# The tail of a two-layer transformer kernel: a loop over stages replaced by an order written out call by call, one of two roundings moved to ScalarE, and the factors of the pairs taken out of rings

## The reference, cut to what matters

```python
scores = einsum('bthd,bshd->bhts', wq, wk) / sqrt(8)
attn   = einsum('bhts,bshd->bthd', softmax(scores), wv)
x      = x + tanh(g_xattn[1]) * (attn @ wo.T + bo)
...
def qlinear(x, w, b):                         # rows of x scaled to -127..127 and rounded
    scale = 127.0 / clip(max(abs(x), -1), EPS)
    xq = clip(round(x * scale), -128, 127)
    return (xq @ wq.T) / (scale * sw) + b     # wq is -1, 0 or 1
h   = layernorm(x, gamma, beta)               # 128 wide
h   = gelu(qlinear(h, w1, b1))                # 512 wide
x   = x + tanh(g_ffn[1]) * qlinear(h, w2, b2)
```

## Time and profile before

| | |
|---|---|
| median of 3 runs | 430.23 us |
| the profiled execution, its time | 430.68 us |
| its span, first to last instruction | 428.9 us |
| granted TensorE clock, mean over the span | 0.976 |
| busy: PE, DVE, ACT, POOL | 90%, 77%, 60%, 53% |
| last exp of the phase starts on ACT | 379.84 us |
| last store is issued | 426.68 us |

### The profile page before, as it was taken

How to read it: one execution, slowest core, us unless ns; L and a number is a source line. 1 busy time by engine, 2 the same in 40 slices (tenths; PEclk the granted TensorE clock), 3 DMA queues, 4 the chain that set the end, 5 groups by cost and what they waited for, 6 DMA issues and landing times. The chain is left out here.

```text
span 428.9 us, 10603 instructions
## 1 busy us (share of the span) xinstructions
PE 383.9 (90%) x3641; PEld 282.8 (66%) x3654; DVE 332.2 (77%) x933; ACT 255.9 (60%) x506; POOL 226.7 (53%) x372
## 2 busy tenths in 40 slices
PE   8799989999999999999999999988888887765765
PEld 7356656666666666786578887856666766654554
DVE  3789998999989998885738874665588888866772
ACT  2478757777777777766542224445777676773252
POOL 4575497566666666632300002773788887656021
PEclk9999999999999999999999999999999999975799
DMA  5889999100000000000000000000000000000011
GB/s 160 245 146 136 135 125 127 14 3 2 2 2 2 2 2 2 0 2 2 2 2 0 0 2 2 0 2 2 2 2 3 2 2 2 2 2 0 16 38 49
DMA packets 61284, 13.29 MB, mean 31 GB/s; under 512 B 51488, under 2 KB 60592, under 8 KB 61232
## 3 DMA queue, kind: packets, MB, share of 16 engines
q1 hardware_dynamic: 59776, 11.94, 18.8%
q10 hardware_dynamic: 1328, 0.66, 0.5%
q0 software_dynamic: 128, 0.00, 0.0%
HBM read 11.55 MB, written 1.05 MB: 29 GB/s over the span
## 5 line engine op out<-in xcount | busy, mean ns | idle before, releaser
L397 POOL TENSOR_TENSOR a_rn<-a_ssq,neghalf 128x8 f32<-128x8 f32 x48 | 79.0, 1655 | 30.1 <-DVE a_ssq L996 25.6
L996 DVE TENSOR_REDUCE a_ssq<-q_home 128x8 f32<-128x512 f32 x48 | 32.3, 673 | 6.4 <-ACT q_home L783 6.3
L486 PE MATMUL a_x<-wkv_a,a_kvT 128*128 128x512 f32 x64 | 34.5, 621 | 0.9 <-ACT kv_home L789 0.8
L91 POOL TENSOR_TENSOR moments<-moments,eps_row 128x1 f32<-128x1 f32 x32 | 6.2, 195 | 54.9 <-DVE moments L86 54.6
L789 ACT ACTIVATE kv_home<-a_x,maskcol 128x512 f32<-128x512 f32 x32 | 21.9, 684 | 18.4 <-PE a_x L486 18.4
L1750 DVE TENSOR_REDUCE b_mx<-b_s 128x16 f32<-128x1024 f32 x16 | 19.6, 1225 | 10.4 <-PE b_s L1461 10.3
L1338 POOL TENSOR_TENSOR b_k<-b_ksb,quad 128x256 f32<-128x256 f32 x32 | 19.0, 614 | 14.3 <-ACT b_ksb L1625 14.3
L1015 DVE TENSOR_REDUCE a_mx<-a_s 128x4 f32<-128x512 f32 x32 | 22.0, 686 | 2.0 <-PE a_s L512 1.9
L413 POOL TENSOR_TENSOR a_yr<-a_ymv,eps_row 128x1 f32<-128x1 f32 x16 | 3.1, 192 | 38.0 <-DVE a_ymv L1039 38.0
L801 ACT ACTIVATE kv_home<-a_m,cols 128x512 f32<-128x512 f32 x32 | 22.0, 686 | 0.8 <-PE a_m L500 0.7
L531 PE MATMUL a_m<-kv_home,p_home 128*64 128x65 f32 x512 | 22.0, 228 | 0.3 <-ACT p_home L811 0.3
(11 more groups left out here) (293 smaller groups left out, 1186.7 us busy)
## 6 DMA issues: line engine op xcount, KB each, us to landing
w_gu<-in_L_ffn_Wg_dram SPq DMA_DIRECT2D x4, 512.0 KB, 9.1
w_gu<-in_L_ffn_Wu_dram SPq DMA_DIRECT2D x4, 512.0 KB, 11.1
w_d<-in_L_ffn_Wd_dram SPq DMA_DIRECT2D x8, 256.0 KB, 7.8
out_dram<-xs SPq DMA_DIRECT2D x8, 128.0 KB, 1.8
xs<-in_x_dram SPq DMA_DIRECT2D x1, 640.0 KB, 11.4
cs<-in_ctx_dram SPq DMA_DIRECT2D x1, 640.0 KB, 10.9
wkv_a<-in_L_xattn_Wkv_dram SPq DMA_DIRECT2D x1, 512.0 KB, 8.4
nat<-in_L_ffn_w_dram SPq DMA_DIRECT2D x2, 256.0 KB, 3.1
```

Of the source, the lines that this page charges most:

```text
L397: nc.gpsimd.tensor_tensor(rn[:, tp, i, :], ssq[:, tp, i, :], neghalf[:, 0:H0], ALU.pow)\
L486: nc.tensor.matmul(p_x[:], kvT[:, tp, b * 2 * S:(b + 1) * 2 * S], wkv_a[:, INNER:2 * INNER], start=True, stop=True).then_inc(vproj_done, 1)
L996: nc.vector.tensor_reduce(ssq[:, tp, i, :], sq[:, i, :].rearrange("p (h d) -> p h d", h=H0), AX.X, ALU.add).then_inc(reduced, 1)
```

## The change

1. In all four loops the stages behind the attention's last exp are cut off, and the calls that remain are written out one by one, in an order of their own for each engine.
2. The two idle matmuls of `turn_hidden` become a call of their own, `keep_busy(j)`. It is called ten times (three times for pair 0, once for each other pair), where before there were eight; the first stands ahead of `up(11)`.
3. Of each pair, the odd tile is rounded by ScalarE (`round_out`), the even one by VectorE as before. `turn_hidden` waits for a semaphore of each.
4. The factors of the second half have a column for each tile (`top2`, `fine2`, `back2`, 128x16) in place of the rings of two pairs, and the waits that guarded the rings are gone.

The number and the size of all other calls is the same.

```diff
+        top2 = sb("top2", [P, NT])
+        fine2 = sb("fine2", [P, NT])
+        back2 = sb("back2", [P, NT])
...
             def hidden_back(j):
                 pool.wait_ge(g_bound, j + 1)
-                wait(pool, x_done, j - 1)
...
-            for s in range(3, NT + 4 + NP):
+            for s in range(3, NT + 3):
...
+            norm_back(12)
+            add_bias(15, 1)
+            add_bias_2(0)
+            inverse_root(13)
+            norm(13, 1)
+            add_bias_2(1)
+            norm_back(13)
+            add_bias_2(2) ... add_bias_2(5), hidden_back(0), add_bias_2(6), hidden_back(1)
+            inverse_root(14), norm(14, 0), hidden_back(2), hidden_back(3), inverse_root(15), norm(15, 1)
+            norm_back(14), hidden_back(4), add_bias_2(7), norm_back(15), hidden_back(5), (6), (7)
...
-            def turn_hidden(j):
+            def keep_busy(j):
                 if j < 2:
                     pe.wait_ge(shifted, NT)
                 wait(pe, gT_ready, j - 1)
                 busy(nc, p_s[:, 2 * (j % 2), 0:256], ident[:], v["wq_a"][:, 0:256], 2)
-                pe.wait_ge(g_rounded, 2 * j + 2)
+
+            def turn_hidden(j):
+                wait(pe, gT_ready, j - 1)
+                pe.wait_ge(g_rounded, j + 1)
+                pe.wait_ge(g_odd_rounded, j + 1)
...
+            def round_out(t):
+                act.wait_ge(g_fine, t // 2 + 1)
+                nc.scalar.activation(hid[:, t, :], hid[:, t, :], ACT.Copy, bias=MAGIC, scale=fine2[:, t:t + 1])\
+                    .then_inc(g_odd_rounded, 1)
...
             def hidden_largest(j):
                 dve.wait_ge(gelu_done, j + 1)
-                wait(dve, g_back, j - 1)
```

More of the change, by code:

```diff
@@ L1572, in _ @@
             pe.wait_ge(zeroed, 3)
-            for s in range(1, NT + 4 + NP):
+            for s in range(1, NT + 1):
                 if s == 3:
@@ L1585, in _ @@
                     up(s - 6, s % 2)
[L1586 to L1589, removed]
                 if exists(s - 3, NT):
@@ L1602, in _ @@
                     mix(s - 2, s % 2, 0)
+            mix(14, 0, 1)
+            keep_busy(0)
+            up(11, 1)
+            probs_T(15, 1, 0)
+            probs_T(15, 1, 1)
+            turn_attention(14, 0)
+            keep_busy(0)
+            keep_busy(1)
+            out_proj(14, 0)
+            turn_norm(12, 0)
+            mix(15, 1, 0)
+            mix(15, 1, 1)
+            keep_busy(0)
+            turn_hidden(0)
+            turn_hidden(1)
+            turn_attention(15, 1)
+            up(12, 0)
+            keep_busy(2)
+            down(0)
+            out_proj(15, 1)
+            down(1)
+            turn_hidden(2)
+            keep_busy(3)
+            turn_hidden(3)
+            down(2)
+            keep_busy(4)
+            turn_norm(13, 1)
+            down(3)
+            up(13, 1)
+            turn_norm(14, 0)
+            turn_hidden(4)
+            turn_norm(15, 1)
+            keep_busy(5)
+            up(14, 0)
+            turn_hidden(5)
+            up(15, 1)
+            keep_busy(6)
+            down(4)
+            down(5)
+            turn_hidden(6)
+            keep_busy(7)
+            turn_hidden(7)
+            down(6)
+            down(7)
         @block.scalar
@@ L1684, in _ @@
                     ternary_out(1, w2_t[:].rearrange("p c k -> p (c k)"))
-            for s in range(2, NT + 2 + NP):
+            for s in range(2, NT + 1):
                 if exists(s, NT):
@@ L1691, in _ @@
                     exp(s - 2, s % 2)
[L1692 to L1695, removed]
                 if exists(s, NT):
@@ L1704, in _ @@
                     norm_out(s - 5, (s - 5) % 2)
[L1705 to L1708, removed]
+            exp(15, 1)
+            gelu(0)
+            gelu(1)
+            attention_out(14, 0)
+            probs_out(15, 0)
+            probs_out(15, 1)
+            norm_out(12, 0)
+            gelu(2)
+            round_out(1)
+            round_out(3)
+            gelu(3)
+            hidden_out(0)
+            hidden_out(1)
+            attention_out(15, 1)
+            gelu(4)
+            round_out(5)
+            gelu(5)
+            round_out(7)
+            hidden_out(2)
+            hidden_out(3)
+            round_out(9)
+            norm_out(13, 1)
+            norm_out(14, 0)
+            round_out(11)
+            gelu(6)
+            norm_out(15, 1)
+            hidden_out(4)
+            hidden_out(5)
+            gelu(7)
+            round_out(13)
+            round_out(15)
+            hidden_out(6)
+            hidden_out(7)
         @block.vector
@@ L1880, in _ @@
                     norm_factors(s - 3)
+            row_stats(13, 1)
+            shift(15, 1)
+            row_moments(13, 1)
+            attend(14, 0)
+            norm_round(12, 0)
+            hidden(11)
+            norm_largest(13, 1)
+            norm_factors(13)
+            hidden_largest(0)
+            hidden_largest(1)
+            output(14, 0)
+            hidden_bound(0)
+            hidden_factor(0)
+            hidden_round(0)
+            hidden_bound(1)
+            hidden_factor(1)
+            hidden_round(2)
+            hidden_largest(2)
+            row_stats(14, 0)
+            row_moments(14, 0)
+            attend(15, 1)
+            hidden_bound(2)
+            hidden_largest(3)
+            hidden(12)
+            hidden_bound(3)
+            hidden_factor(2)
+            hidden_round(4)
+            output(15, 1)
+            row_stats(15, 1)
+            hidden_largest(4)
+            norm_largest(14, 0)
+            hidden_factor(3)
+            hidden_round(6)
+            final(0)
+            row_moments(15, 1)
+            norm_round(13, 1)
+            final(1)
+            norm_factors(14)
+            norm_round(14, 0)
+            hidden_bound(4)
+            hidden_factor(4)
+            hidden_largest(5)
+            norm_largest(15, 1)
+            hidden_round(8)
+            norm_factors(15)
+            norm_round(15, 1)
+            hidden_bound(5)
+            hidden_factor(5)
+            hidden(13)
+            final(2)
+            hidden_round(10)
+            hidden(14)
+            hidden_largest(6)
+            hidden(15)
+            final(3)
+            hidden_bound(6)
+            hidden_factor(6)
+            hidden_round(12)
+            hidden_largest(7)
+            hidden_bound(7)
+            hidden_factor(7)
+            hidden_round(14)
+            final(4)
+            final(5)
+            final(6)
+            final(7)
 _INS = ["x", "ctx_1024", "mask_BxS2_bk0", "g_xattn", "g_ffn",
```

59 lines of the change are left out of this document (32 added, 27 removed).

## The result

The changed kernel takes 416.19 us (median of 4 runs, 415.6 to 416.67) against 429.9 us (429.12 to 431.01, 4 runs): ratio 0.9678, 95% interval 0.9652 to 0.9704. The forecast was 414.5 us, with a range of 411.5 to 419.5. The profiled execution took 416.1 us with a span of 414.3, against the 413.1 that the prediction worked out.

A forecast was written before the change was run, and what follows sets the result against it. Behind the last exp, a PE-ACT ring and a low clock bound the kernel, no engine being full. Span 412.6 from the walk plus 0.5 gives 413.1; plus 1.8 gives 414.9; less 0.45 gives 414.5 us, range 411.5 to 419.5.

The forecast's parts named there:

- The walk: Four engine orders behind the last exp followed call by call; last down ends at 409.7 us, span 412.6.
- the 0.5 us for calls with several waits: Estimated allowance over the chain for calls with several waits; raises the span from 412.6 to 413.1 us.
- In the walk add_bias_2 runs in POOL's pauses: nothing.: POOL's additions, 0.72 us each, were said to run in POOL's pauses and cost nothing.
- the rounding on ACT: Eight odd-tile roundings on ScalarE, taken at 0.54 us between starts, with bounds of 0.48 and 0.70.
- The gain on DVE: DVE is freed of eight roundings of 0.39 us, 3.1 us.
- rival (a): Clock still falls once, near 381.7 us; turn_hidden(0) ends 1.8 later, time 416 to 419; chance 0.28 with (d).
- Rival (b): The low clock stays behind 381.7 us and PE's calls double; 431 us, no gain or slightly slower; chance 0.03.
- The first fills PE's hole: The first of ten keep_busy calls fills PE's idle hole, from 379.87 to 380.8 us.
- the ring: PE's turn_hidden(j + 1) behind down(j) waits for ACT's copy; 3.53 us a pair, PE idle 1.03 each time.
- the load of DVE: DVE's calls from 380.92 us add up to 27 us, the largest of the engine sums.
- Rival (c): Copies with a factor by row reload the table, ten switches of 1.28 us; 422 us; chance 0.07 with longer stalls.
- Rival (d): A late call stalls a queue, likeliest DVE at norm_largest(15); 1 to 2 us each, 416 to 419; 0.28 with (a).

The follow-up runs named there:

- e5: Changed kernel with four of POOL's additions, add_bias_2(4) to (7), moved behind later hidden_back calls; 414.08 us, ratio 0.9619.
- e6: Changed kernel with both tiles of each pair rounded by VectorE and round_out gone; 421.88 us, ratio 0.9776.
- e2: Changed kernel with none of its ten keep_busy calls; 416.09 us, ratio 0.9675.
- e1: Changed kernel without its first keep_busy(0), the one ahead of up(11); 415.91 us, ratio 0.9663.
- e9: Kernel before with turn_hidden(j + 1) ahead of down(j) and without the idle matmuls in turn_hidden; 425.45 us, ratio 0.9842.
- e10: Kernel of e9 with the odd tile rounded on ScalarE ahead of hidden_out and columns in place of rings, still in loop order; 430.6 us, ratio 0.9984.
- e4: Kernel before with two lines exchanged, so turn_hidden(j + 1) stands ahead of down(j); 426.13 us, ratio 0.9879.
- e8: Kernel before, its ring kept, without the two idle matmuls in turn_hidden; 426.45 us, ratio 0.9885.
- e11: Order of e5 with row_moments(15) earlier, final(3) later, turn_hidden(6) ahead of down(5), keep_busy(6) and (7) left out; 416.32 us, ratio 0.9633.
- e3: Kernel before with one more pair of idle matmuls, behind mix(14, 1) and ahead of up(11); 429.8 us, ratio 0.9978.

## Why the prediction was right

**The amount.** 15.8 us of span were forecast, 14.6 came. Of these, 0.45 came ahead of the table load, by chance. In the stretch: forecast 48.0 - (413.1 - 380.92) = 15.8, measured 14.1, so 1.7 us too much.

**The walk held, call by call.** Shifted by the 0.45, it had DVE's rounding of pair 1 end at 387.05 (388.0 measured), turn_hidden(3) at 395.15 (396.43, where PE's next call starts), gelu(7) start at 403.2 (404.91), and the last `down` end at 409.25 (411.42). The kernel is behind the walk by 0.95, 1.3, 1.7 and 2.2 us. 0.9 of the first and 0.5 between the second and the third, 1.5 together by e5, are DVE calls lengthened by POOL. The remaining 0.7 are about what was allowed: the 0.5 us for calls with several waits, and 0.2 for the longer roundings on ACT (below). This last division is an estimate; no run separates it.

**The step that failed:** "In the walk add_bias_2 runs in POOL's pauses: nothing." It does run in POOL's pauses, but on top of DVE's bound and roundings, and costs 1.5 us (e5). The earlier trace rows had its 0.72 us, and the trace before shows the same kind of DVE call, the rounding of a norm tile, at more than twice its length while POOL works (its L1338 runs from 373.76 to 374.94 us), against 0.28 at 380.37:

```profile
374.42 0.61 DVE L1806 TENSOR_SCALAR b_hr<-b_hn,b_fine 128x128 f32<-128x128 f32 x1
```

**A term that was off:** the rounding on ACT was taken at 0.54 between starts, with 0.70 as the upper bound. It is 0.63: 0.7 us more over eight calls, within the bounds, and by the prediction's own share of a third 0.2 at the end. The prediction says that no row shows a Copy with a factor by row. The trace before has 32 at each of two lines; L801 is one, from PSUM, and the next call starts 0.59 us behind it (181.22):

```profile
180.63 0.69 ACT L801 ACTIVATE kv_home<-a_m,cols 128x512 f32<-128x512 f32 x1
```

The gain on DVE, 3.1, was right within the spread (e6: 3.05, or 2.85 from `output(14)` on).

**Right for less than it seemed: the clock.** The range was made mostly from a clock that falls (rival (a), 1.8 us and more). The clock did stay up in the profiled execution; but e2 shows that its fall, at that place, costs 0.2 us or nothing, since PE has room while DVE paces. So for the clock the time would have come out right either way. Rival (b), the clock down for good, is not what e2 shows either: it came back at about 390 us, after a stretch in which PE was busy 3.00 of 3.00 us. "The first fills PE's hole" is true and not needed (e1).

**The reasons, sorted by the runs.** Turn ahead of down and no idle matmuls, in the old loops: 48.0 to 41.0, 7.0 us (e9). The written orders with both roundings on DVE, and the columns in place of rings: 41.0 to 36.9, 4.1 us (e6). The odd tile on ScalarE: 36.9 to 33.8, 3.05 us, and not in the loop's order as e10 has it. The prediction had the ring and the load of DVE; it did not see that the old idle matmuls alone cost 4.8 us, which stood in the earlier trace rows as 0.92 of a pair's 3.53. It also gave the rings of factors no price, where they set the pace of e4, e8 and e9. The step from e9 to e6 also puts the ten idle calls in; by e2 these are worth 0.2 us or nothing, so the sum stands. How the 4.1 us divide was not measured: the rings are in it (0.4 us a pair were idle in e9), the rest of the order, and the clock. e9's clock is 0.50 from about 383.3 to 403.7 us, and PE's calls on its chain in that time, 3.0 us between 384.0 and 387.7 and one turn of 1.96, would be 2.5 us shorter at the upper clock. That is an estimate of the most that the clock can hold of the 4.1.

**Rival (c)**, a table load for each rounding, did not come: one load behind 378 us in the trace. **Rival (d)**, a queue that stalls, did not come either: between 390 and 401 us PE's longest pause is 0.94 us, and DVE waits 0.30 at norm_largest(15), where the walk had 0.35.

## What to carry to other kernels

Where no engine is full and yet each pair takes the same time, follow the chain once around: a ring of two engines is cut by exchanging two calls, and the next ring then shows (e9). Moving work to an idler engine helps only if the order there lets it go when its input is ready; e10 turned a gain of 3 us into a loss of 6, part of it the clock's. Count an engine's work in its pauses as free only after looking at which calls of its neighbours it lengthens (e5), and put idle matmuls in for the clock only where PE's own calls are on the chain and the idle ones are not.

## What the runs showed of the hardware that was not expected

**A clock that falls in another phase, in some executions.** In five profiles (e4, e6, e9, e10, e11) the granted clock drops between 190 and 210 us, in a part that no kernel here changes, with PE busy throughout. e11 first, then the changed kernel, which does not show it:

```profile
190.00:200.00 10.00, 10.00 (x63) 7.59 (x61) 4.37 (x16) 7.24 (x14) 4.16 (x11) 0.93 0.01 3
200.00:210.00 10.00, 9.85 (x39) 4.65 (x38) 5.99 (x20) 3.93 (x9) 0.37 (x1) 0.73 0.00 1
```

```profile
200.00:210.00 10.00, 9.85 (x61) 5.08 (x61) 8.06 (x30) 6.11 (x13) 2.16 (x2) 1.00 0.01 2
```

In these five the table load comes at 382.71 to 384.01 us, in the other kernels' at 379.36 to 380.92, save e3 (382.86, with a clock of 1.00 there). e3 lost its time at the start: its clock averages 0.91 in the first 20 us, where the kernel before has 1.00, and a table load near 192 us already comes 1.96 us later (194.58 against 192.62). What the fall costs can also be read from the runs of e11: the three with a mean clock of 0.996 or 1.0 took 413.84, 413.84 and 415.25 us, those with 0.986 to 0.988 took 417.4 to 418.0. Medians of four to six runs of these kernels mix the two, and so can differ by more than an edit does; the stretch leaves this fall out. The Trainium skill, "TensorE: Matmul & The Clock Gate", section "What's actually happening", calls the moment of a change of the clock variable from run to run, because the counting is not tied to the kernel's start. That would move the moment of a fall; why the clock falls at all where PE is busy 10.00 of 10.00 us, no run here shows.
